# Weighing the values once per block: four tile-packed matmul groups together instead of one per unit, in two attention pipelines

## What is computed

```python
x = _layernorm(x + _L0_attn_ref(x, ...))            # self-attention, MLP
x = _layernorm(x + _L0_xattn_ref(x, ctx, ctx, ...)) # cross-attention
x = _layernorm(x + _L0_ffn_ref(x, ...))             # mixture of experts, top 2 of 8
x = _layernorm(x + _L1_attn_ref(x, ...))            # causal attention
x = _layernorm(x + _L1_xattn_ref(x, ctx, ctx, ...)) # recurrence over the sequence
x = _layernorm(x + _L1_ffn_ref(x, ...))             # switch mixture of experts

# inside each attention, per sequence and head:
scores = einsum('bhqd,bhkd->bhqk', q, k) / sqrt(8)  # masked
attn = softmax(scores, axis=-1)
ctx = einsum('bhqk,bhkd->bhqd', attn, v)            # the weighing of the values
```

## Time and profile before

| | us |
|---|---|
| median of 3 runs | 1362.21 (1361.73 to 1365.23) |
| span of the profiled execution | 1363.6 |
| encode | about 0 to 660 of the span |
| decode | about 820 to 1140 of the span |

### The profile page before, as it was taken

The page is one execution under the profiler, slowest core; times in us unless marked ns, Lnnn a source line. Parts: engine busy times, 40 slices in busy tenths (PEclk is TensorE's granted clock), DMA queues, the critical chain, the costliest instruction groups (busy, mean ns, idle before and its releaser), DMA issues. The chain is left out here.

```text
span 1363.6 us, 31925 instructions
## 1 busy us (share of the span) xinstructions
PE 1199.7 (88%) x10209; PEld 819.7 (60%) x10209; DVE 1041.1 (76%) x3184; ACT 863.3 (63%) x2474; POOL 553.3 (41%) x831
## 2 busy tenths in 40 slices
PE   3789999999999999988489988999999979999796
PEld 2456666666666666654256655555555556777796
DVE  3477888887888888885678867999999975666365
ACT  2677887878887878864246643666666654543464
POOL 1233334425353434432400017556655311556377
PEclk9999999999999999987589988999999999999899
DMA  6100000000000000000122222013100000000673
GB/s 267 52 17 9 17 15 21 29 17 29 15 31 17 26 19 17 13 15 13 53 67 81 82 71 98 24 39 79 43 24 18 5 1 3 17 17 25 178 209 92
DMA packets 71490, 63.54 MB, mean 47 GB/s; under 512 B 10510, under 2 KB 61586, under 8 KB 70688
## 3 DMA queue, kind: packets, MB, share of 16 engines
q1 hardware_dynamic: 62768, 45.27, 11.5%
q0 software_dynamic: 6400, 12.63, 3.0%
q10 hardware_dynamic: 2160, 3.60, 0.8%
HBM read 43.00 MB, written 18.98 MB: 45 GB/s over the span
## 5 line engine op out<-in xcount | busy, mean ns | idle before, releaser
L777 PE MATMUL e_bank_turned<-c_matrices,e_probs 128*128 128x128 f32 x1024 | 166.0, 286 | 16.2 <-ACT e_probs_t L1009 9.0
L703 POOL TENSOR_TENSOR e_rstd<-e_var_eps,c_minus_half 128x1 f32<-128x1 f32 x128 | 71.0, 570 | 253.6 <-DVE e_var_eps L1050 253.3
L1009 ACT ACTIVATE e_probs_t<-e_bank_turned 128x512 f32<-128x512 f32 x256 | 154.9, 605 | 16.0 <-PE e_bank_turned L777 14.5
L1137 DVE TENSOR_REDUCE e_neg_max<-e_bank_scores 128x4 f32<-128x512 f32 x160 | 109.5, 684 | 50.6 <-PE e_bank_scores L820 50.2
L777 PEld LDWEIGHTS e_bank_turned<-c_matrices,e_probs 128*128 128x128 f32 x1024 | 116.7, 145 | 39.9 <-issue 16.1
L787 PE MATMUL e_bank_mix<-e_probs_t,e_values 128*32 128x128 f32 x2048 | 113.2, 294 | 15.5 <-ACT e_probs_t L1009 15.1
L968 ACT ACTIVATE e_probs<-e_scores,e_neg_max 128x128 f32<-128x128 f32 x384 | 123.2, 410 | 1.1 <-DVE e_neg_max L1173 1.1
L1784 ACT ACTIVATE d_probs_t<-d_bank_turned 128x512 f32<-128x512 f32 x128 | 77.4, 605 | 65.9 <-PE d_bank_turned L1661 65.9
L963 ACT ACTIVATE e_probs<-e_scores 128x512 f32<-128x512 f32 x128 | 82.1, 642 | 42.0 <-DVE e_scores L1170 41.4
L706 POOL TENSOR_TENSOR e_k_by_place<-e_q_k_k,c_matrices 128x512 f32<-128x512 f32 x64 | 66.6, 1040 | 102.6 <-DVE e_q_k_k L1181 102.6
L1766 ACT ACTIVATE d_probs<-d_scores 128x512 f32<-128x512 f32 x128 | 80.8, 631 | 38.9 <-DVE d_scores L1807 38.5
(11 more groups left out here) (328 smaller groups left out, 3267.4 us busy)
## 6 DMA issues: line engine op xcount, KB each, us to landing
streamed<-in_s_up SPq DMA_DIRECT2D x36, 258.0 KB, 3.4
sorted_rows<-scratch_sorted SPq DMA_DIRECT2D x72, 64.0 KB, 1.8
scratch_expert_out<-m_y SPq DMA_DIRECT2D x72, 64.0 KB, 1.5
sorted_rows<-scratch_sorted SPq DMA_DIRECT2D x40, 65.0 KB, 3.0
e_x_in<-in_x SPq DMA_DIRECT2D x32, 64.0 KB, 1.9
e_ctx_in<-in_ctx SPq DMA_DIRECT2D x32, 64.0 KB, 2.1
up<-in_m_wgv SPq DMA_DIRECT2D x1, 2048.0 KB, 7.5
up_b<-in_m_bgv SPq DMA_DIRECT2D x1, 2048.0 KB, 14.1
```

What stands on the lines that cost most here:

```text
L777: last = nc.tensor.transpose(turned_bank[:, j * P:(j + 1) * P], pr[k % 3][:, j, :], c["ident"][:])
L1009: nc.scalar.activation(pt[k % 2][:], turned_bank[:], ACT.Copy).then_inc(probs_t_ready, 1)
L1137: nc.vector.tensor_reduce(nmax[k % 4][:], bank, AX.X, ALU.max, negate=True).then_inc(max_ready, 1)
```

## The change

In both pipelines PE weighs a block's four units in one go. In encode this happens at the second place of the next block, `place % G == 1`, where the fourth unit was weighed before; it stands ahead of the turn of that tick as before. `weigh` now waits once, for ACT's copy of the fourth unit, for the values and for the copy of the mix of the block before, issues 4 x 4 matmuls, and counts `mixed` up once. The weighings of the first three units go from the three ticks ahead. `pt` has four buffers instead of two, since four units' turned probabilities are kept until then. ACT waits for `mixed` by blocks. In decode the same is done at `g == 1`.

```diff
@@ -777,15 +777,16 @@
                     last = nc.tensor.transpose(turned_bank[:, j * P:(j + 1) * P], pr[k % 3][:, j, :], c["ident"][:])
                 last.then_inc(probs_turned, 1)
 
-            def weigh(att, n, g, k):
-                pe.wait_ge(probs_t_ready, k + 1)
-                if g == 0:
-                    pe.wait_ge(act_read, (ACT_TURNS["q1v1", n] if att else ACT_TURNS["mix0_v0", n - 1]) + 1)
-                    if k:
-                        pe.wait_ge(mix_copied, k // G)
-                for j in range(G):
-                    last = nc.tensor.matmul(mix_bank[32 * j:32 * j + VC, g * P:(g + 1) * P], lhsT=va[att][n % 3][:, G * g + j, :],
-                                            rhs=pt[k % 2][:, j * P:(j + 1) * P], start=True, stop=True)
+            def weigh(att, n, k):
+
+                pe.wait_ge(probs_t_ready, k + G)
+                pe.wait_ge(act_read, (ACT_TURNS["q1v1", n] if att else ACT_TURNS["mix0_v0", n - 1]) + 1)
+                if k:
+                    pe.wait_ge(mix_copied, k // G)
+                for g in range(G):
+                    for j in range(G):
+                        last = nc.tensor.matmul(mix_bank[32 * j:32 * j + VC, g * P:(g + 1) * P], lhsT=va[att][n % 3][:, G * g + j, :],
+                                                rhs=pt[(k + g) % 4][:, j * P:(j + 1) * P], start=True, stop=True)
                 last.then_inc(mixed, 1)
 
             def bank_free(k):
@@ -873,12 +874,11 @@
                         pe.wait_ge(x3_ready, n - LATE + 1)
                         last = nc.tensor.transpose(act_bank[:, P:2 * P], x3[(n - LATE) % 10][:], c["ident"][:])
                     last.then_inc(act_written, 1)
-                if place % G == 1 and unit_at(tick - 2):
-                    weigh(*unit_at(tick - 2), UNIT_NUMBER[tick - 2])
+                if place % G == 1 and unit_at(tick - 5):
+                    att, n, _ = unit_at(tick - 5)
+                    weigh(att, n, UNIT_NUMBER[tick - 5])
                 if unit_at(tick - 1):
                     turn(UNIT_NUMBER[tick - 1])
-                if place % G != 1 and unit_at(tick - 2):
-                    weigh(*unit_at(tick - 2), UNIT_NUMBER[tick - 2])
                 if place == 6 and unit_at(tick + 2):
                     for g in LIGHT:
                         distance(UNIT_NUMBER[tick + 2], g)
@@ -954,7 +954,7 @@
             for tick in ENCODE_TICKS:
                 for att, offset in ((0, 6), (1, 42)):
                     if (n := at(tick, offset)) is not None:
-                        act.wait_ge(mixed, UNIT_NUMBER[tick - 6] + G)
+                        act.wait_ge(mixed, UNIT_NUMBER[tick - 6] // G + 1)
                         nc.scalar.activation(ot[att][:], mix_bank[:], ACT.Copy).then_inc(mix_copied, 1)
                 if unit_at(tick):
                     k = UNIT_NUMBER[tick]
@@ -1006,7 +1006,7 @@
                 if unit_at(tick - 1):
                     k = UNIT_NUMBER[tick - 1]
                     act.wait_ge(probs_turned, k + 1)
-                    nc.scalar.activation(pt[k % 2][:], turned_bank[:], ACT.Copy).then_inc(probs_t_ready, 1)
+                    nc.scalar.activation(pt[k % 4][:], turned_bank[:], ACT.Copy).then_inc(probs_t_ready, 1)
                 if (i := group_at(tick, 67)) is not None:
                     act_route(nc, act, r, i)
             write_pads(act, c["zeros"], table, scr["sorted0"], 1)
...
@@ -1661,17 +1661,16 @@
-            def weigh(u):
-
-                b, g = divmod(u, G)
-                pe.wait_ge(probs_t_ready, u + 1)
-                if g == 0:
-                    pe.wait_ge(v_ready, b + 1)
-                    if b:
-                        pe.wait_ge(mix_copied, b)
-                for j in range(G):
-                    last = nc.tensor.matmul(mix_bank[32 * j:32 * j + VC, g * P:(g + 1) * P], lhsT=va[b % 4][:, G * g + j, :],
-                                            rhs=pt[u % 2][:, j * P:(j + 1) * P], start=True, stop=True)
+            def weigh(b):
+
+                pe.wait_ge(probs_t_ready, G * b + G)
+                pe.wait_ge(v_ready, b + 1)
+                if b:
+                    pe.wait_ge(mix_copied, b)
+                for g in range(G):
+                    for j in range(G):
+                        last = nc.tensor.matmul(mix_bank[32 * j:32 * j + VC, g * P:(g + 1) * P], lhsT=va[b % 4][:, G * g + j, :],
+                                                rhs=pt[g][:, j * P:(j + 1) * P], start=True, stop=True)
                 last.then_inc(mixed, 1)
 
             pe.wait_ge(buffers_set, 2)
@@ -1685,12 +1684,10 @@
                             pe.wait_ge(shifted, b * G + bank + 1)
                             mask(b + 1, bank)
                     scores(b + 1)
-                if g == 1 and 2 <= tick < UNITS_ALL + 2:
-                    weigh(tick - 2)
+                if g == 1 and 0 < b <= BATCH:
+                    weigh(b - 1)
                 if 1 <= tick <= UNITS_ALL:
                     turn(tick - 1)
-                if g != 1 and 2 <= tick < UNITS_ALL + 2:
-                    weigh(tick - 2)
                 if g == 2 and 0 <= b < BATCH - 1:
                     for bank in (0, 1):
                         pe.wait_ge(shifted, b * G + bank + 1)
@@ -1759,7 +1756,7 @@
             act.wait_ge(buffers_set, 2)
             for tick in TICKS:
                 if (b := due(tick, 6)) is not None:
-                    act.wait_ge(mixed, G * b + G)
+                    act.wait_ge(mixed, b + 1)
                     nc.scalar.activation(ot[b % 2][:], mix_bank[:], ACT.Copy).then_inc(mix_copied, 1)
                 if 0 <= tick < UNITS_ALL:
                     act.wait_ge(shifted, tick + 1)
@@ -1781,7 +1778,7 @@
                     nc.scalar.activation(xT_all[:, :, b], act_bank[:, 0:P], ACT.Copy).then_inc(x5T_ready, 1)
                 if 1 <= tick <= UNITS_ALL:
                     act.wait_ge(probs_turned, tick)
-                    nc.scalar.activation(pt[(tick - 1) % 2][:], turned_bank[:], ACT.Copy).then_inc(probs_t_ready, 1)
+                    nc.scalar.activation(pt[(tick - 1) % G][:], turned_bank[:], ACT.Copy).then_inc(probs_t_ready, 1)
             act.wait_ge(x5T_ready, BATCH)
 
         @block.vector
```

The ring of `pt` in both phases:

```diff
-                            tiles("probs_t", [P, G * P]))
+                            tiles("probs_t", [P, G * P], 4))
```

## The result

| | us, median (lowest to highest) | span of the profiled run | mean clock |
|---|---|---|---|
| before | 1365.12 (1361.73 to 1370.61, 6 runs) | 1363.6 | 0.964 |
| after | 1374.55 (1372.72 to 1377.3, 6 runs) | 1375.4 | 0.954 |

The ratio is 1.0067, with a 95% interval of 1.0044 to 1.0089: 9 us slower. The forecast was 1350, and its range ended at 1364. It had started from a median of 1362.21, of three runs; with six the kernel before stands at 1365.12.

A forecast was written before the change was run, and what follows sets the result against it. Encode was taken as bound by PE, decode as shared by nearly full PE and DVE. 1363.6 - 19.1 (encode) + 3 (decode) + 4 (clock) = 1351.5; with the runs' median 1.4 below the span, 1350 us, range 1336 to 1364.

The forecast's parts named there:

- The group: PE's four weighings in a row: 1.02 us, 0.66 more than the single weighing there; bounds 1.02 and 1.44.
- (c): Rival: next weighing's weights don't get in behind running ones, each weighing in the group costs 0.36; 1385 us; chance 0.08.
- (d): Rival: a weight load of 0.11 before each of eight rounds, a group of 1.9 us, kernel 1424 us; chance 0.02.
- Encode's steady part: 27 frames: 15 clean ones 0.79 us shorter, 12 long ones 0.6 shorter; 19.1 us less in all.
- The clock: Encode's long frames: PE's longer wait before the group lowers the clock, three times 1.3, +4 us; bounds 0 and 8.
- The ramps at both ends wait for dependences; I take 0 (+-2).: Encode's start and end: no change in time, 0 us, give or take 2.
- Decode: About 30 blocks: L1725 waits for ACT's copy of the turned mix, +0.10 each, +3 us; bounds -0.29 to +0.37 a block.
- Rival (b): Gain used up, 1357 to 1367 us: clock falls in all five frames and the ends, or decode pays 0.37; chance 0.18.

## Why the prediction was wrong

**The group: right.** Forecast 1.02, measured 1.01 us, and the turn behind it 0.66. More rounds of weights don't stop each other: in the group of 194.99 the eight rounds start 0.11 us apart, and the turn comes 0.20 behind the last. That rules out rivals (c) and (d). The Trainium skill has the rule that a load overlaps running matmuls only for another row group (TensorE: Matmul & The Clock Gate, Part 3: Packing small matmuls, row/col tiling). By the prediction's estimate it would have made 1.9 us of the group; the trace disagrees with its 1.01.

**Encode's steady part: right, and a little more.** The first half was to change by +0.08 and did by +0.07 (7.59 to 7.66), the second by -0.87 and did by -0.97 (10.64 to 9.67). Long frames won 0.75 to 1.1 each instead of 0.6. Without stalls the 27 frames won 23 us and more instead of 19.1.

**The clock: wrong place.** PE waits 1.7 us ahead of the group in the five long frames, as forecast, but the granted clock stays at 2.4 GHz behind it. PE's timeline, and the windows behind it:

```profile
213.88 1.08 PE L788 MATMUL e_bank_mix<-e_probs_t,e_values 128*32 128x128 f32 x32 [1.71 <-ACT e_probs_t L1009]
```

```profile
213.90:216.90 3.00, 3.00 (x50) 2.80 (x51) 2.81 (x8) 2.73 (x10) 2.00 (x3) 1.00 0.01 3
580.90:583.90 3.00, 3.00 (x15) 3.00 (x16) 1.03 (x4) 2.09 (x7) 0.55 (x1) 0.50 0.01 3
```

Only the sixth, where the wait has grown to 2.36 us (579.76), falls to 1.2 GHz, as it did before. The term of +4 measured 0 there. The price of a fall was right: in the run with the group behind the turn, PE waits 1.81 us in one long frame, the clock falls to 1.2 GHz, and the frame takes 20.31 us where its like take 18.7. The place was not. And the length of a wait doesn't decide alone: over the 14 traces with the group ahead of the turn the wait of 2.36 us was followed by a fall 9 times of 14, and with the old order that of 1.65 us 3 times of 4. The clock was lost at the ends instead.

**The step that failed: "The ramps at both ends wait for dependences; I take 0 (+-2)."** This term was +13, and 16 in the result's own trace (7.6 and 8.4). At the ends PE waits for dependences indeed, but the change takes work out of PE's idle time there and puts it behind the last copy. That lengthens the chain, by 0.4 to 1.8 us at the start and some 4 at the end, and it leaves PE idle for longer, with which the granted clock stays at 1.2 GHz: 4 to 7 us at the start. The prediction priced the clock in the middle and not here. It had looked at one frame in the middle only, and let the sentence stand in for a reading. One block of the first 80 us would have shown the idle time that the weighings fill.

**Decode: right mechanism, wrong size.** L1722 (L1725 before) waits for ACT's copy of the turned mix, as forecast; moving this copy alone takes the wait away and 0.36 us off the block. But a block costs +0.28, not +0.10, nearer the upper bound of 0.37. The turn came 0.37 later, as worked out. The rest had been taken as if a wait cost nothing beyond itself: from the copy's end to L1722 are 0.14 us (950.46 to 950.60) where 0.06 was reckoned, and from L1722 to the scores 0.95 where it was 0.86, since the matmuls behind a wait come more slowly. Over decode that is 7.4 instead of 3.

**Not foreseen: the stalls,** +11 us on the chips that have them, the one of the result among them. Their cause stays open.

The sum for a chip without: -23 - 0 + 13 + 8 = -2, and after's ratios there are 1.0005 and 0.9992. With the stalls it is +9, and the ratios are 1.0067 and 1.0060. So the sign of the result is that of the stalls; the change itself is worth nothing as made. Rival (b), the gain used up, at 0.18, comes nearest: its 1357 to 1367 hold the two runs without stalls. Its reasons were right in part. The clock fell at the ends and not in the five frames, and decode paid 0.28 and not 0.37. The result itself, 1374.55, lies beyond (b), and none of the rivals had its reason.

## What to carry to other kernels

Packing small matmuls of one tile form together pays where the engine is the bound (0.9 us a frame here), and costs where it waits: in the ramps of a pipeline, where only one stream runs, leave the small pieces in the gaps that they fill. The longer link is the smaller part of that cost at the start here, and the low clock that goes with the longer gaps the larger. Ask of a group not only what it costs but what stands behind it: the turn behind the group cost decode 0.28 us a block, and with the two exchanged the same group won 0.33. And read the start and the end of a phase with the same care as its middle; what was lost there was over half of what 27 steady frames won.

## What the runs showed of the hardware

- In two of the changed kernel's four runs PE's count of a group that ended between POOL's two indirect DMAs came 1.6 us after the modelled end instead of 0.045, ten times of ten; in the other two, on another chip and at the same distances to 10 ns, never. The turns that end in such a place come in time (0.015 us). On the chip of one of the two, single weighings of 8 matmuls were 0.45 us late as well.
- A wait of 1.7 us of PE in encode's steady part was never followed by a lower granted clock (70 waits in 14 traces), one of 1.8 once of six times, one of 2.36 in 9 of 14. At the start shorter waits (0.7 to 0.8), one after the other, stood with a clock of 0.50. Twelve traces with groups at the start had 13.7 to 27.3 us at 1.2 GHz there, and reached the same L924 at 98.8 to 105.5 us.
- Behind a wait PE's fp32 matmuls come at 0.14 instead of 0.11 us (950.60 to 950.74), here 0.09 us in all up to the scores.
- Chips differ by more than small changes are worth: before had medians of 1361.9 to 1368.4 us.
